# Gate logits computed with the weights held and transposed back, in a fused S4, retention and top-1 attention tower

## The reference

```python
gating = jax.nn.softmax(x @ W_gate.T, axis=-1)      # x: layer-normed h, W_gate: 16 x 512
idx = jnp.argmax(gating, axis=-1)
indicator = jax.nn.one_hot(idx, H, dtype=gating.dtype)
top1_val = jnp.max(gating, axis=-1, keepdims=True)
qkv = x @ W_qkv.T
q, k, v = jnp.split(qkv, 3, axis=-1)
k_shared = jnp.einsum('bth,bthd->btd', indicator, k)
v_shared = jnp.einsum('bth,bthd->btd', indicator * top1_val, v)
att = jnp.einsum('bhqd,bkd->bhqk', q, k_shared) * (1.0 / math.sqrt(hd))
# causal softmax over k, then att @ v_shared
```

## Time and profile before

| | us |
|---|---|
| three runs | 1315.25, 1316.46, 1320.2 |
| profiled execution | 1319.74 |
| its span, first to last instruction | 1318.0 |
| PE busy | 1227.0 |
| DVE busy | 723.5 |
| ACT busy | 559.1 |
| POOL busy | 518.9 |
| mean granted PE clock | 0.98 |

### The profile page before, as it was taken

The page is one execution under the profiler, slowest core; times in us unless marked ns, Lnnn a source line. Parts: engine busy times, 40 slices in busy tenths (PEclk is TensorE's granted clock), DMA queues, the critical chain, the costliest instruction groups (busy, mean ns, idle before and its releaser), DMA issues. The chain is left out here.

```text
span 1318.0 us, 22927 instructions
## 1 busy us (share of the span) xinstructions
PE 1227.0 (93%) x8280; PEld 1016.7 (77%) x8280; DVE 723.5 (55%) x1360; ACT 559.1 (42%) x1769; POOL 518.9 (39%) x722
## 2 busy tenths in 40 slices
PE   0389999999999999699999999989999999999997
PEld 0368888888888888577877887878888788887875
DVE  7686655666666532455555445435464554645544
ACT  3344333444433321434343332224555555454546
POOL 2757666766676641333333233120321213122121
PEclk9999999999999999999999999889899999999999
DMA  4132222222222225966656535153252706436061
GB/s 155 66 119 96 105 103 114 95 104 105 102 112 91 112 88 190 313 186 209 211 173 176 153 116 145 48 120 82 48 110 52 161 15 148 89 74 137 6 133 34
DMA packets 63359, 154.78 MB, mean 117 GB/s; under 512 B 9616, under 2 KB 26128, under 8 KB 61712
## 3 DMA queue, kind: packets, MB, share of 16 engines
q1 hardware_dynamic: 63248, 153.33, 39.7%
HBM read 67.19 MB, written 56.62 MB: 94 GB/s over the span
## 5 line engine op out<-in xcount | busy, mean ns | idle before, releaser
L1682 ACT ACTIVATE probs<-psum,row_max 128x128 f32<-128x128 f32 (+1 forms) x384 | 142.9, 388 | 48.6 <-DVE row_max L1848 36.7
L1848 DVE TENSOR_REDUCE row_max<-psum 128x2 f32<-128x384 f32 (+1 forms) x128 | 79.2, 619 | 82.4 <-PE psum L2079 43.8
L1010 ACT ACTIVATE square_scratch<-psum 128x128 f32<-128x128 f32 x192 | 50.7, 274 | 172.8 <-PE psum L1243 172.8
L1979 POOL TENSOR_TENSOR h_rows<-h_rows,y_normed 128x512 f32<-128x512 f32 x24 | 30.7, 1281 | 228.2 <-DVE y_normed L1865 228.2
L1956 POOL TENSOR_TENSOR picked_rows<-picked_rows 128x768 f32<-128x768 f32 (+1 forms) x64 | 61.1, 954 | 104.3 <-DVE picked_rows L1830 100.6
L1183 POOL TENSOR_TENSOR rr<-ss,consts_r 128x3 f32<-128x3 f32 x64 | 13.2, 206 | 195.8 <-ACT square_scratch L1010 192.7
L712 PE MATMUL psum<-m,basis 128*128 128x64 f32 x384 | 48.9, 284 | 43.6 <-POOL basis L664 43.6
L1856 DVE COPY raw_f<-psum 128x512 f32<-128x512 f32 x64 | 44.2, 691 | 80.4 <-PE psum L2092 80.3
L683 POOL TENSOR_TENSOR stage<-stage 128x512 f32<-128x512 f32 x48 | 81.6, 1718 | 14.5 <-DVE stage L565 14.5
L712 PEld LDWEIGHTS psum<-m,basis 128*128 128x128 f32 x384 | 49.6, 203 | 45.7 <-issue 43.6
L1682 ACT ACTIVATION_READ_ACCUMULATOR probs<-psum,row_max 128x1 f32 x384 | 80.5, 210 | 0.0
(11 more groups left out here) (269 smaller groups left out, 3594.6 us busy)
## 6 DMA issues: line engine op xcount, KB each, us to landing
qk<-stage SPq DMA_DIRECT2D x24, 512.0 KB, 2.6
v<-stage SPq DMA_DIRECT2D x24, 512.0 KB, 2.6
g<-gate_rows SPq DMA_DIRECT2D x24, 512.0 KB, 2.8
qk_rows<-qk SPq DMA_DIRECT2D x16, 512.0 KB, 7.3
q_stack_even<-q_t_high SPq DMA_DIRECT2D x32, 224.0 KB, 5.5
q_stack_even<-q_t_low SPq DMA_DIRECT2D x32, 224.0 KB, 6.7
q_stack_odd<-q_t_high SPq DMA_DIRECT2D x32, 224.0 KB, 5.4
q_stack_odd<-q_t_low SPq DMA_DIRECT2D x32, 224.0 KB, 6.7
```

The costliest lines, as they stand in the source:

```text
L1010: last = nc.scalar.activation(sqs[:, h % 2, t], psum[:, OB[h % 2], t * RV:(t + 1) * RV], ACT.Square, accum_out=ss[:, h % 2, t:t + 1])
L1682: last = nc.scalar.activation(pr[:, g % 2, c], psum[:, SB[g % 3], c], ACT.Exp, bias=mx[:, g % 3, x:x + 1], accum_out=dsum[:, t, h:h + 1])
L1848: V.reduce_max(mx[:, g % 3, 0:nh], psum[:, SB[g % 3], 0:nh * w].rearrange("p (h n) -> p h n", h=nh), AX, negate=True).then_inc(s_max.sem, 1)
L1979: G.tensor_tensor(h, h, yn[:, (NT * i + t) % 2].rearrange("p h f -> p (h f)"), ALU.add).then_inc(added.sem, 1)
```

## The change

The logits are computed with the gate weights as the stationary operand. For each of the 4 chunks of channels one matmul has the 32 columns of `gw` (high and low) as weights and streams all 384 columns of `xhi`, and one has the 16 high columns as weights and streams `xlo`: 8 matmuls in place of 24. The result has logits on 32 partitions and tokens along the row. ACT copies it to SBUF (`logits_evac`, 32 x 384, into a tile `logits_t` that takes the place of an unused gap), and PE turns it back in three transposes (`logit_rows`), into the same bank behind the first 384 columns, where DVE reads it as before.

PE's transposes stand behind the first q projection of step 0, or, for pair 0, behind the second half of tile 1's output projection. ACT's copy stands ahead of the exponentials at step 0, or, for pair 0, at the end of stage q. DVE's operations and their order are the same.

```diff
@@ scalar(), end of stage q @@
         f["x_split"](0, 2)
+        f["logits_evac"](0)
@@ last(), stage q, PE @@
             f["logits"](0)
             wo(i, 1, 0)
             wo(i, 1, 1)
+            f["logit_rows"](0)
             f["q_proj"](0, 0)
             wo(i, 2, 0)
@@ stage f @@
-    sb("gap_f", [P, 384])
+    lgT = sb("logits_t", [P, TP])
...
+        def logits_evac(i):
+            act.wait_ge(lgt_sum.sem, lgt_sum.at(i, 1))
+
+            act.wait_ge(lg_sum.sem, lg_sum.at(i - 1, 1))
+            nc.scalar.activation(lgT[0:2 * FH, :], psum[0:2 * FH, lg_bank(i), 0:TP], ACT.Copy).then_inc(lgt_out.sem, 1)
...
         def step(i, n, back, ahead, beyond):
             g = NS_F * i + n
+            if n == 0 and ahead:
+                logits_evac(i + 1)
             if g + 1 < LAST:
                 exps(g + 1)
...
-            both = psum[:, lg_bank(i), 0:NT * 2 * FH].rearrange("p (t s f) -> p t s f", t=NT, s=2)
+            both = psum[:, lg_bank(i), TP:TP + NT * 2 * FH].rearrange("p (t s f) -> p t s f", t=NT, s=2)
...
         def logits(i):
             pe.wait_ge(gw_split, 2)
             pe.wait_ge(x_low.sem, x_low.at(i, NT))
+            out = lambda m: psum[0:m, lg_bank(i), 0:TP]
+            for k in range(KC):
+                mm(out(2 * FH), gw[:, k].rearrange("p s f -> p (s f)"), xhi[:, k, :], start=k == 0, stop=False,
+                   skip_group_check=True)
+                last = mm(out(FH), gw[:, k, 0], xlo[:, k, :], start=False, stop=k == KC - 1, skip_group_check=True)
+            last.then_inc(lgt_sum.sem, 1)
+
+        def logit_rows(i):
+            pe.wait_ge(lgt_out.sem, lgt_out.at(i, 1))
             for t in range(NT):
-                ts, o = cols(t), t * 2 * FH
-                for k in range(KC):
-                    mm(psum[:, lg_bank(i), o:o + 2 * FH], xhi[:, k, ts], gw[:, k].rearrange("p s f -> p (s f)"),
-                       start=k == 0, stop=False, skip_group_check=True)
-                    last = mm(psum[:, lg_bank(i), o:o + FH], xlo[:, k, ts], gw[:, k, 0], start=False, stop=k == KC - 1,
-                              skip_group_check=True)
+                o = TP + t * 2 * FH
+                last = nc.tensor.transpose(psum[:, lg_bank(i), o:o + 2 * FH], lgT[0:2 * FH, cols(t)],
+                                           ident[0:2 * FH, 0:2 * FH])
             last.then_inc(lg_sum.sem, 1)
...
                 if n == 0:
                     pe.wait_ge(v_picked.sem, v_picked.at(i, 3))
                     q_proj(j, 0)
+                    logit_rows(j)
```

More of the change, by code:

```diff
@@ L1461, in stage_f @@
     x_low = Signal(sem("x2_low_ready"), NT)
+    lgt_sum = Signal(sem("logits_t_summed"), 1)
+    lgt_out = Signal(sem("logits_t_evacuated"), 1)
     lg_sum = Signal(sem("logits_summed"), 1)
@@ L1635, in scalar @@
     def scalar(act):
-        for s in (normed, x_high, lg_exp, q_high, kt_out, probs, pt_out_a, yt_out):
+        for s in (normed, x_high, lgt_out, lg_exp, q_high, kt_out, probs, pt_out_a, yt_out):
             s.prime(act)
@@ L1751, in run @@
             y_evac(PAIRS - 1, 2)
-        return {"gate_weight": gate_weight, "weight": weight, "norm": norm, "x_split": x_split, "run": run}
+        return {"gate_weight": gate_weight, "weight": weight, "norm": norm, "x_split": x_split, "logits_evac": logits_evac,
+                "run": run}
     def vector(dve):
@@ L2005, in tensor @@
     def tensor(pe):
-        for s in (x_sum, lg_sum, q_sum, k_sum, v_sum, kt_sum, s_sum, pt_sum, y_sum, yr_sum):
+        for s in (x_sum, lgt_sum, lg_sum, q_sum, k_sum, v_sum, kt_sum, s_sum, pt_sum, y_sum, yr_sum):
             s.prime(pe)
@@ L2247, in run @@
             y_rows(PAIRS - 1, 2)
-        return {"x_transposes": x_transposes, "logits": logits, "q_proj": q_proj, "run": run}
+        return {"x_transposes": x_transposes, "logits": logits, "logit_rows": logit_rows, "q_proj": q_proj, "run": run}
     return Stage(sync, scalar, vector, gpsimd, tensor)
```

## The result

The changed kernel takes 1304.09 us (median of 6 runs, 1302.37 to 1305.04) against 1315.94 (6 runs, 1313.62 to 1320.2); ratio 0.9891, 95% interval 0.9872 to 0.9911. The profiled execution took 1305.04 us, span 1303.3, mean granted clock 0.991 where it was 0.98. Forecast was 1304.0, range 1299 to 1311. The medians differ by 11.9 us; the forecast was worked out from the profiled execution of the kernel before, 1319.74.

The account below looks back on a forecast made before the run. PE was taken to set the pace, busy 1227.0 of 1318.0 us. Savings of 5.2 + 1.8 + 1.5 + 6.4 + 0.8 = 15.7 us off the profiled 1319.74 gave 1304.0 us, range 1299 to 1311.

Parts of the forecast that it names:

- six clean pairs: Pairs 2 to 7 at full clock: shorter logits run less the added transposes, 0.87 us each, 5.2 us.
- pair 1's run and transposes: Pair 1's logits at 1.2 GHz: 5.08 us replaced by 2.63 plus 0.64 for transposes, 1.8 us gained.
- pair 0: End of the middle stage: PE stalls 1.0 us for DVE's addition before tile 2, yet gains 1.5 us.
- the clock: Dense matmuls keep PE's granted clock up in and behind the logits runs of pairs 2, 4 and 6: 6.4 us returned.
- the early rise: In pair 1, denser work could lift PE's low clock one step earlier: 0 to 1.6 us, 0.8 taken.
- The new run: Eight 384-column logits matmuls on PE, priced like the q projection at 0.178 us each, 1.43 us at full clock.
- The transposes: Three added 32x128 logit transposes on PE, 0.38 us at full clock, 0.64 us in pair 1.
- The bound of 0.7: Upper bound for the three logit transposes on PE: 0.40 us plus a 0.29 us restart behind a wait.
- ACT's copy: 384-column logits copy ahead of step 1's exponentials, 0.49 us, hidden with 2.0 us of slack before PE's transposes.
- Rival A: Clock falls near the logits runs stay; gain only 7.0 us, from the median to 1309.5 us; chance 0.18.
- The two accounts of the median: Profiled execution lies 3.28 us above the median; if from two extra clock falls, the median also ends at 1304.
- The range: Whole kernel, 1299 to 1311 us: lower by cheaper terms (5 us together), upper to take in Rival A.

Follow-up runs that it names:

- copy_mid: Changed kernel with ACT's logits copy behind the exponentials of step 1 instead of ahead of them; 1303.22 us, ratio 0.9885.
- copy_late: Changed kernel with ACT's logits copy behind step 1's exponentials and two more ACT copies of 1536 columns; 1318.85 us, ratio 0.9995.
- rows_early: Changed kernel with pair 0's three logit transposes moved between the halves of tile 1's output projection; 1303.47 us, ratio 0.9889.
- the two narrow kernels: Changed kernel with 24 extra unread 32-column matmuls, ahead of the logits of pairs 2 to 7 or of the third q projection; ratios 1.0068 and 1.0039.
- narrow_2: Changed kernel with 24 extra unread 32-column matmuls ahead of the third q projection in pairs 1 to 6; 1323.14 us, ratio 1.0039.
- full_rows: Changed kernel with 128x128 logit transposes in place of 32x128, ACT copying all 128 partitions; 1302.32 us, ratio 0.9879.

## Why the prediction was right, point by point

The forecast time and the measured one differ by 0.1 us, which is partly luck. The forecast takes 15.7 us off the profiled execution, whose time lies 3.8 above the median of its six runs, and it meets the other kernel's median. The profiled spans differ by 14.7 us; the run of logits of pair 0 starts at 838.82 where it started at 837.7, in stages that no edit touches, so the change took 15.8 us off the rest. Forecast was 15.7. Term by term, in the order of the forecast's sum, the traces give 4.2 + 2.0 + 1.6 + 6.4 + 1.8 = 16.0 for its 5.2 + 1.8 + 1.5 + 6.4 + 0.8: six clean pairs at 0.70, pair 1's run and transposes (5.08 - 2.56 - 0.49), pair 0, the clock, the early rise.

- **The new run**: 1.43 us forecast, 1.39 measured in pair 0, spaced 0.174, and 1.49 in pairs 2 to 7. The q projection was the right row. At 1.2 GHz 2.56 (886.96 - 884.40) against 2.63.
- **The transposes** were the mis-sized term: 0.38 forecast, 0.49 measured. With the run's 0.06 a clean pair is 0.70 faster, not 0.87, which loses 6 x 0.17 = 1.0 us against the forecast. The bound of 0.7 held it. I had allowed for a restart behind a wait; a fixed part is real, but it comes with the change of shape.
- **ACT's copy**: 0.48 us, slack 2.1 us against 2.0. Right, and copy_mid and copy_late show it from both sides.
- **Pair 0**: stall 0.84 us against 1.0, gain 1.6 against 1.5. Right, and in rows_early the stall goes once the transposes, and with them DVE's chain, come earlier.
- **The clock**: the term of 6.4 us. Pairs 2 to 6 returned all of it: 58.13, 57.11 and 57.08 became 54.78, 54.79 and 54.76. In all ten profiles with dense logits (among them the kernel before with wide ones; copy_late, with its long waits, is not counted) no pair between 2 and 7 had a fall; in the three with sparse stretches there were three, three and two.
- **Pair 1's early rise**: 0.8 us forecast between 0 and 1.6. The stretch from pair 1 to pair 2 fell from 948.54 - 889.72 = 58.82 to 55.76, 3.06 us. Of this the run of pair 2 gave 3.23 - 1.49 = 1.74, the transposes took 0.49, and 1.8 us are left for the rise: its first q projection already ran at full clock, from 889.36, and took about 2.2 us where it had taken 3.94. That is 1.0 us more than forecast, as much as the run and the transposes took beyond theirs: two errors of a microsecond cancel in the sum.
- **The two accounts of the median** (that the profiled execution stood 3.3 us high because of two falls more) are not shown by any run, since only one execution was profiled. What fits it: the kernel before spread over 6.6 us in 6 runs, the changed one over 2.7. In the 42 further executions of the kernel before that stand beside the experiments, 14 took less than 1317 us, at mean granted clocks of 0.982 to 0.985, the other 28 more than 1318, at 0.977 to 0.982. So the executions that took longer are those at the lower clock, whose falls no trace shows. It also means that its median depends on how many of each a set of six holds: beside the experiments it is 1319.15 to 1319.94, and the changed kernel, in the one set that has both, is 14.2 us faster, not 11.9.
- **The range**: its lower end was given as 5 us of cheaper terms; by the figures beside it they are about 4: 0.12 in eight runs, 0.3 seven times, and 0.8.

Rival A (the falls stay) is refuted by the wide logits and the two narrow kernels. The Trainium skill (TensorE: Matmul & The Clock Gate, Why this matters for your kernels) ties the fall to idle gaps of PE; here it fell with PE listed as busy all the time, in the earlier trace rows and in narrow_2, so the measurement decides against reading that rule as complete.

## What to carry to other kernels

Matmuls with few moving columns and full weights cost 0.11 us each here, the same with 16 columns as with 128, and they may also take PE's clock down for what stands behind them (in three of six pairs here): look at the granted clock in windows right behind such a stretch, not at the busy share. Which operand is held decides both; where it can't be swapped, streaming the same columns several times over costs 0.04 us a run here and returned 6 us. When a result has to come back through another engine, place the copy where the round trip has two microseconds of other work on PE, because a stall there is paid as a wait and sometimes, behind three of seven here, a second time in the clock.

## What was not expected of the hardware

- A kernel that streams four times the columns in its logits is 0.4% faster (0.9959), only because the clock stays up.
- Transposes of 32 rows follow each other at 0.06 us, but the first one's weight load stands still for 0.25 us behind 128-row matmuls. The Trainium skill (TensorE: Matmul & The Clock Gate, LDWEIGHTS) gives a 32x128 load the time of a 128x128 one, by its formula an estimated 107 ns. The traces agree that the two are alike and list both longer, 0.137 us in the changed kernel and 0.139 in full_rows. But the transposes start 0.06 us apart with 32 rows and 0.11 apart with 128, so what PE pays for one is not the listed load, and the larger cost was at the two changes of shape.
- PE waits of 1.14 us, each behind a dense projection, were followed by a fall of the clock in two of six pairs of copy_late; in copy_mid, the same kernel without the waits, there was none.
